# Four mixture-of-experts feed-forwards: the experts' weights are copied to all partitions by GpSimd instead of by a one-hot product

## What is computed

```python
comb = top_k_weights(x @ router)              # tokens x experts, zero outside the top 2 (L0: top 4 of 128)
for e in experts:                             # L1: 16, L2: 8, L3: 8; hidden width 128, 128, 176
    h = silu(x @ Wg[e]) * (x @ Wu[e])
    out += comb[:, e:e+1] * (h @ Wd[e])
out += shared(x)                              # the same without a weight; L2: weighted by a sigmoid gate
```

## Time and profile before

| | |
|---|---|
| time, median of 3 runs | 1829.1 us (1828.53 to 1836.51) |
| the profiled execution | 1830.67 us, span of its instructions 1828.8 us, mean granted TensorE clock 0.984 |
| TensorE, VectorE, ScalarE, GpSimd busy | 95%, 61%, 39%, 12% |
| L0's feed-forward | from 491.5 to 556.9 us |
| L1's | from 695.4 to 803.0 us |
| L2's | from 1195.0 to 1261.6 us |
| L3's, with the store | from 1741.7 to 1828.8 us |

### The profile page before, as it was taken

One profiled execution on the slowest core, in us unless ns is written; L12 is line 12 of the kernel. 1 busy time (PEld: TensorE's weight loads), 2 busy tenths in 40 slices (PEclk: granted clock), 3 DMA queues, 4 the chain that ended last, 5 costly groups with the idle time before them and its releaser, 6 DMA issues. The chain is left out here.

```text
span 1828.8 us, 35508 instructions
## 1 busy us (share of the span) xinstructions
PE 1732.9 (95%) x15270; PEld 1161.0 (63%) x15270; DVE 1106.8 (61%) x1938; ACT 720.3 (39%) x1213; POOL 218.0 (12%) x384
## 2 busy tenths in 40 slices
PE   8999999999998889998989999999999999999998
PEld 4584367777664655655447777755366757777755
DVE  1824578888456763245568888534455358888532
ACT  2222256666312331123246666411354246666411
POOL 0122500000000000000420000000166000000000
PEclk9999999999999889998999999998999999999999
DMA  6302010000210021040020000050200220000010
GB/s 213 112 1 94 1 70 2 2 2 2 87 84 1 2 76 37 1 147 18 1 87 2 2 2 2 2 233 3 52 7 1 104 82 2 2 2 2 2 56 10
DMA packets 11789, 73.45 MB, mean 40 GB/s; under 512 B 3483, under 2 KB 5019, under 8 KB 7125
## 3 DMA queue, kind: packets, MB, share of 16 engines
q1 hardware_dynamic: 11634, 71.19, 10.7%
HBM read 70.73 MB, written 0.46 MB: 39 GB/s over the span
## 5 line engine op out<-in xcount | busy, mean ns | idle before, releaser
L941 ACT ACTIVATE arena<-ps,softmax_stats 128x1500 f32<-128x1500 f32 x168 | 253.8, 1511 | 218.7 <-DVE softmax_stats L1004 216.5
L863 PEld LDWEIGHTS ps<-arena,ctx_pos 125*64 125x64 f32 x4608 | 222.3, 137 | 58.4 <-issue 57.6
L850 PE MATMUL ps<-ident,arena 64*125 64x64 f32 x4032 | 237.9, 270 | 12.9 <-ACT arena L941 8.0
L850 PEld LDWEIGHTS ps<-ident,arena 64*125 64x125 f32 x4032 | 228.7, 185 | 31.5 <-issue 30.5
L863 PE MATMUL ps<-arena,ctx_pos 125*64 125x128 f32 (+1 forms) x4608 | 240.5, 262 | 0.0
L781 PE MATMUL ps<-ctx_feat,arena 64*128 64x500 f32 x1008 | 232.2, 589 | 6.6 <-issue 3.3
L948 ACT COPY arena<-ps 125x512 f32<-125x512 f32 x336 | 172.5, 600 | 70.2 <-PE ps L850 70.2
L199 PE MATMUL ps<-arena 128*128 128x256 f32 x736 | 176.0, 386 | 8.7 <-DVE arena L1242 3.0
L1015 DVE TENSOR_SCALAR arena<-arena,softmax_stats 128x1500 f32<-128x1500 f32 x168 | 168.3, 1002 | 5.9
L199 PEld LDWEIGHTS ps<-arena 128*128 128x128 f32 x736 | 138.4, 191 | 47.1 <-issue 17.7
L1139 PE MATMUL ps<-x_feat,arena 128*128 128x448 f32 (+1 forms) x416 | 166.1, 544 | 0.0
(11 more groups left out here) (279 smaller groups left out, 1978.3 us busy)
## 6 DMA issues: line engine op xcount, KB each, us to landing
ctx_pos<-in_ctx SPq DMA_DIRECT2D x1, 3000.0 KB
arena<-in_L1f_gate SPq DMA_DIRECT2D x1, 2304.0 KB, 11.1
arena<-in_L1f_up SPq DMA_DIRECT2D x1, 2304.0 KB, 16.1
arena<-in_L1f_down SPq DMA_DIRECT2D x1, 2304.0 KB, 7.8
arena<-in_L0a_Wq SPq DMA_DIRECT2D x1, 2048.0 KB, 9.6
arena<-in_L0a_Wc SPq DMA_DIRECT2D x1, 2048.0 KB, 11.0
arena<-in_L0x_Wq SPq DMA_DIRECT2D x1, 2048.0 KB, 12.6
arena<-in_L0x_Wo SPq DMA_DIRECT2D x1, 2048.0 KB, 12.9
```

What stands on the lines that cost most here:

```text
L850: m = nc.tensor.transpose(c.ps[0:LP, turn_bank(i, k, r), n * 64:(n + 1) * 64], probs[i % 2][e][rows, l * LP:(l + 1) * LP], c.ident[rows, r ...
L863: m = nc.tensor.matmul(y[r * 64:(r + 1) * 64, lo:hi], c.ctx_pos[:, j, l, e, :], pT[i % 2][:, lo // 64:hi // 64, LT * e + l, :], start=(l = ...
L941: nc.scalar.activation(probs[i % 2][e].rearrange("p (k l) -> p k l", k=3), sc[e], ACT.Exp, bias=low[:, i % 4, e:e + 1], accum_out=total[:, ...
```

## The change

The one-hot products, the tables and their loads go. In their place:

- *Rounds of four.* comb (in L1 to L3) is laid out so that expert e has column 32 * (e % 4) of round e // 4, the rest being cleared once. Turning a round (four transposes, `widen(r)`) puts the weights of its four experts on partitions 0, 32, 64 and 96 of a PSUM bank, and VectorE copies it to SBUF (`wide_out(r)`). L1 has 4 rounds, L2 3, L3 2. In L0 comb is turned as before, and a round is one product of `mixed` (the mixing table with the same spacing) with combT; 2 rounds. Rounds 0 and 1 go ahead of the loop on TensorE, further ones behind `down(0)` and `down(1)`. On VectorE round 0 goes ahead of the first gated chunk and each further one behind one.
- *Copies by GpSimd.* For each weighted chunk one `partition_broadcast` copies the expert's row (448 columns, from partition 0, 32, 64 or 96) to the 128 partitions of one of several SBUF tiles (8, 13, 5 and 11 of them in L0 to L3). A chunk with two experts takes two, the second over the first partitions, after a wait for the first. A tile is used again when its chunk has been gated.
- VectorE's second multiplication reads that tile instead of PSUM.

```diff
+    experts = 8 if mixing else f.cols if kind == "L2" else E
+    R = (experts + 3) // 4
+    combT = c.at(W + 1920, NT)
+    wideT = [c.at(W + (1920 + 448 * r if r < 2 else 3680 + 448 * r), NT) for r in range(R)]
+    if mixing:
+        wideT = wideT[1:] + [c.at(W + 4576, NT)]
+        comb = c.at(22256, 512).rearrange("p (j e) -> p j e", j=J)
+        mixed = c.at(22000, 256).rearrange("p (r m) -> p r m", r=R)
+    else:
+        comb = c.at(22000, J * R * 128).rearrange("p (j r m) -> p j r m", j=J, r=R)
+    tiles = [c.at(at, NT) for at in f.tiles]
...
+
+        k = f.chunks[n][2]
+        a, b = (min((128 * k + p) // f.width, experts - 1) for p in (0, 127))
+        return [(b, 128)] + ([(a, f.width * (a + 1) - 128 * k)] if a != b else [])
...
-            nc.gpsimd.memset(comb, 0.0).then_inc(*padded.next())
+            nc.gpsimd.memset(mixed if mixing else comb, 0.0).then_inc(*padded.next())
...
+            for i, n in enumerate(weighted):
+                if i >= len(tiles):
+                    pool.wait_ge(hid_in.handle, hid_in.at(weighted[i - len(tiles)] + 1))
+                tile = tiles[i % len(tiles)]
+                for step, (e, rows) in enumerate(of_chunk(n)):
+                    pool.wait_ge(wide_in.handle, wide_in.at(e // 4 + 1))
+                    if step:
+                        pool.wait_ge(bc_half.handle, bc_half.last())
+                    row = 32 * (e % 4)
+                    nc.gpsimd.partition_broadcast(tile[0:rows], wideT[e // 4][row:row + 1], channels=rows).then_inc(
+                        *(bc_in if step + 1 == len(of_chunk(n)) else bc_half).next())
...
-            def weights(n):
-
-                if n in weighted:
-                    pe.wait_ge(combT_in.handle, combT_in.at(1))
-                    m = nc.tensor.matmul(c.ps[:, bank(n) + 2, 0:NT], spread[:, f.chunks[n][2], :], combT,
-                                         start=True, stop=True)
-                    m.then_inc(*bc_mm.next())
+            def widen(r):
+
+                if r >= 2:
+                    pe.wait_ge(wide_in.handle, wide_in.at(r - 1))
+                bank = c.ps[:, 7 - 3 * (r % 2), :]
+                if mixing:
+                    m = nc.tensor.matmul(bank[:, 0:NT], mixed[:, r, :], combT, start=True, stop=True)
+                else:
+                    for j in range(J):
+                        m = nc.tensor.transpose(bank[:, j * 128:(j + 1) * 128], comb[:, j, r, :], c.ident[:])
+                m.then_inc(*wide_mm.next())
...
             pe.wait_ge(comb_in.handle, comb_in.at(1))
-            for j in range(J):
-                t = nc.tensor.transpose(c.ps[:, 7, j * 128:(j + 1) * 128], comb[:, j, :], c.ident[:])
-            t.then_inc(*comb_t.next())
+            if mixing:
+                for j in range(J):
+                    t = nc.tensor.transpose(c.ps[:, 7, j * 128:(j + 1) * 128], comb[:, j, :], c.ident[:])
+                t.then_inc(*comb_t.next())
+                pe.wait_ge(combT_in.handle, combT_in.at(1))
+            widen(0)
+            widen(1)
             arrived_late()
-            weights(0)
-            weights(1)
             for n in range(N):
                 if n > 0 or not mixing:
                     down(n)
-                if n + 2 < N:
-                    if n > 0 or not mixing:
-                        gate_up(n + 2)
-                    weights(n + 2)
+                if 2 <= n + 2 < R:
+                    widen(n + 2)
+                if n + 2 < N and (n > 0 or not mixing):
+                    gate_up(n + 2)
...
                 dve.wait_ge(s.dve_chain.handle, s.dve_chain.last())
                 V.tensor_scalar(mix[:, 0:8], mix[:, 0:8], mix[:, 8:9], scale, ALU.mult, ALU.mult).then_inc(*s.dve_chain.next())
                 dve.wait_ge(s.dve_chain.handle, s.dve_chain.last())
-                V.tensor_copy(spread[:, 0:8, :], mix[:, 0:8].unsqueeze(2).broadcast_to([128, 8, 128])).then_inc(*s.dve_chain.next())
+                V.tensor_copy(mixed.rearrange("p r (g m) -> p r g m", g=4)[:, :, :, 0],
+                              mix[:, 0:8].rearrange("p (r g) -> p r g", r=R)).then_inc(*s.dve_chain.next())
...
                 if n in weighted:
                     V.tensor_tensor(sl, up, sl, ALU.mult).then_inc(*s.dve_chain.next())
                     dve.wait_ge(s.dve_chain.handle, s.dve_chain.last())
-                    dve.wait_ge(bc_mm.handle, bc_mm.at(weighted.index(n) + 1))
-                    V.tensor_tensor(h, valid(c.ps[0:m_, bank(n) + 2, 0:NT]), valid(sl), ALU.mult).then_inc(*hid_in.next())
+                    i = weighted.index(n)
+                    dve.wait_ge(bc_in.handle, bc_in.at(i + 1))
+                    V.tensor_tensor(h, valid(tiles[i % len(tiles)][0:m_]), valid(sl), ALU.mult).then_inc(*hid_in.next())
...
-            V.tensor_tensor(comb[:, :, 0:E], ex, spr(small[:, 12:16]), ALU.mult).then_inc(*comb_in.next())
+            if mixing:
+                V.tensor_tensor(comb, ex, spr(small[:, 12:16]), ALU.mult).then_inc(*comb_in.next())
+            else:
+                V.tensor_tensor(comb[:, :, 0:E // 4].rearrange("p j r (g m) -> p j r g m", g=4)[:, :, :, :, 0],
+                                ex.rearrange("p j (r g) -> p j r g", g=4),
+                                small[:, 12:16].rearrange("p (j r g) -> p j r g", r=1, g=1).broadcast_to([128, J, E // 4, 4]),
+                                ALU.mult).then_inc(*comb_in.next())
             dve.wait_ge(comb_in.handle, comb_in.last())
...
+            if mixing:
+                dve.wait_ge(comb_t.handle, comb_t.at(1))
+                V.tensor_copy(combT.rearrange("p (b t) -> p b t", b=B),
+                              c.ps[:, 7, :].rearrange("p (b t) -> p b t", b=B)[:, :, 0:T]).then_inc(*combT_in.next())
+                dve.wait_ge(combT_in.handle, combT_in.last())
...
+            def wide_out(r):
+                dve.wait_ge(wide_mm.handle, wide_mm.at(r + 1))
+                bank = c.ps[:, 7 - 3 * (r % 2), :]
+                V.tensor_copy(valid(wideT[r]), valid(bank[:, 0:NT]) if mixing else
+                              bank.rearrange("p (b t) -> p b t", b=B)[:, :, 0:T]).then_inc(*wide_in.next())
+
+            wide_out(0)
             for n in range(1 if mixing else 0, N):
                 gated(n)
+                r = n if mixing else n + 1
+                if r < R:
+                    wide_out(r)
             norm_vector(c, s, dve, last)
 
 
...
-                          29696, 32256, 34816, 3, 35584, 22000, 35840),
+                          29696, 32256, 34816, 3, 35584, 35840, 128, [27000 + 448 * i for i in range(6)] + [22784, 23232]),
-                          6144, 10752, 25780, 18, 32448, 30400, 32480),
+                          6144, 10752, 25780, 18, 32448, 32480, 128, [448 * i for i in range(13)]),
-                          29696, 32256, 34816, 10, 37376, 22000, 37400),
+                          29696, 32256, 34816, 10, 37376, 37400, 128, [27200 + 448 * i for i in range(5)]),
-                          29696, 33280, 0, 14, 37448, 22000, 24064),
+                          29696, 33280, 0, 14, 37448, 24064, 176, [8000 + 448 * i for i in range(11)]),
-    if name != "L0_ffn":
-        n = {"L1_ffn": 16, "L2_ffn": 10, "L3_ffn": 11}[name]
-        d["spread"] = (tag + "_spread", c.at(f.spread, n * 128))
-                    "L2_xattn_last": 2, "L3_xattn_first": 3, "L3_xattn_next": 1, "L3_xattn_last": 2, "L0_ffn": 5, "L1_ffn": 6, "L2_ffn": 4, "L2_ffn_late": 1, "L3_ffn": 3, "L3_ffn_late": 2,
+                    "L2_xattn_last": 2, "L3_xattn_first": 3, "L3_xattn_next": 1, "L3_xattn_last": 2, "L0_ffn": 5, "L1_ffn": 5, "L2_ffn": 4, "L3_ffn": 3, "L3_ffn_late": 1,
-                fl["L1_ffn"], "down", "router", "spread", "extra")))
+                fl["L1_ffn"], "down", "router", "extra")))
-            feed_forward(c, "L2_ffn", spec["L2_ffn"], pick(fl["L2_ffn"], "spread"),
+            feed_forward(c, "L2_ffn", spec["L2_ffn"], [],
-            feed_forward(c, "L3_ffn", spec["L3_ffn"], pick(fl["L3_ffn"], "spread", "down"), nothing, out)
+            feed_forward(c, "L3_ffn", spec["L3_ffn"], pick(fl["L3_ffn"], "down"), nothing, out)
```

More of the change, by code:

```diff
@@ L1060, with __init__ @@
 class Experts:
-    def __init__(self, cols, experts, top, chunks, gate_tiles, gate, up, down, downs, router, spread, extra):
+    def __init__(self, cols, experts, top, chunks, gate_tiles, gate, up, down, downs, router, extra, width, tiles):
         self.cols, self.experts, self.top, self.chunks = cols, experts, top, chunks
         self.hidden, self.gate, self.up, self.down, self.downs = gate_tiles, gate, up, down, downs
-        self.router, self.spread, self.extra = router, spread, extra
+        self.router, self.extra, self.width, self.tiles = router, extra, width, tiles
 def feed_forward(c, name, f, now, prefetch, store=None, meanwhile=None):
@@ L1073, in feed_forward @@
     kind, E, last = name[:2], f.experts, store is not None
+    mixing = kind == "L0"
```

(31 more changed lines are left out.)

## The result

The changed kernel took 1820.28 us (median of 4 runs, 1804.6 to 1823.68); the kernel before took 1832.8 us beside it (4 runs, 1828.53 to 1842.64). The ratio is 0.9896, with a 95% interval of 0.9847 to 0.9945. So it is faster, by 12.5 us and not by 26.7, and it lies above the range that ended at 1812. The profiled execution took 1821.77 us (span 1819.7), to be set beside 1830.67 of before: 8.9 us less.

The account below looks back on a forecast made before the run. TensorE, 95% busy, bounds the kernel: 31.5 - 1.9 (ends) - 1.5 (rounds) - 1.4 (L0) - 0.2 (L2) + 0.2 (L1 attention) = 26.7 us gained, so 1804.0 us profiled, 1802.4 median; range 1797 to 1812.

Parts of the forecast that it names:

- The products (31.5 us): Feed-forward loops: 42 of 45 one-hot products leave TensorE's path at 0.75 us each, 31.5 us gained.
- Ends and rounds (1.9, 1.5): TensorE waits 0.47 us at four stage ends, 1.9 lost; three later rounds at 0.5 us in L1 and L2, 1.5 lost.
- L0 (1.4): L0's start: VectorE must copy round 0's product before gated(1), so down(1) comes later; net 1.4 us lost.
- The copy's price: One GpSimd copy of 448 columns: taken as 0.6 us, from plain copies (0.58) and an all-reduce (14 at most).
- The 54 us: One GpSimd copy by the skill page's reduction figure; the change would then cost over 2 ms.
- L2's start (0.2 lost): First copy and one SBUF hold of 0.6 us before down(0): 0.2 us lost, between 0.4 gained and 0.8 lost.
- all three loads are hidden: GpSimd's code loads in L0, L2 and L3 finish before the first copy can start, by 3 us at least.
- rival (b): Code loads begin only when input is ready and land on the path: gain 13.4, 1815.7 us; 4%.
- The sum: Whole kernel: all terms give 26.7 us gained, from the profiled 1830.67 to 1804.0, or 1802.4 for the median.
- The likeliest case: Whole kernel: the forecast itself, 1802.4 us, 4 us either way for clock dips and L2's hold; 80%.
- rival (d): TensorE's clock dips once per feed-forward after new idle times, 6.4 us lost, 8 with a fifth: 1810.4 us; 7%.

Follow-up runs that it names:

- the first repetition: The changed kernel run once more with no edit: 1815.63 us (7 runs), ratio 0.9906.
- the last six: The changed kernel, unedited, run again beside the kernel before on one chip: 1804.12 us (6 runs), ratio 0.9861.
- eight copies: The changed kernel with each GpSimd copy made eight times in sequence, each waited for: 1959.47 us (one execution).

## Why the prediction was wrong, point by point

**The products (31.5 us).** Right: 4.74 us per chunk and nothing in the loop waits. L1's feed-forward shows it by itself: forecast 16 x 0.75 = 12.0, less 0.47 and two rounds, 10.5; measured 9.1 with a fall of the clock that before did not have, and 10.7 without one (107.62 to 96.88). L3: 11 x 0.75 less 0.47 is 7.8; measured 6.2 and another 1.7 of clock, 7.9.

**Ends and rounds (1.9, 1.5).** Right: 0.43 us at L3's end for 0.47, and 0.44 us for a round of L1 (four transposes at 703.42, the next gate products at 703.86) for 0.5.

**L0 (1.4).** Right: the stage is 3.3 us shorter, and 7 x 0.75 - 0.47 - 1.4 is 3.4. The timeline shows the order that I worked out, answering to the earlier trace rows:

```profile
506.00 1.77 PE L1177 MATMUL ps<-arena 128*128 128x448 f32 x4 [0.78 <-DVE arena L1343]
...
507.13 0.62 DVE L1350 COPY arena<-ps 128x448 f32<-128x448 f32 x1 [1.18 <-PE ps L1177]
507.67 0.62 DVE L1278 TENSOR_TENSOR arena<-ps,arena 128x448 f32<-128x448 f32 x1
...
508.34 1.99 PE L199 MATMUL ps<-arena 128*128 128x256 f32 x8 [0.57 <-DVE arena L1278]
```

**The copy's price.** Between the ends of 0.58 and 14 us I took 0.6, and it is 0.66: the plain copy was the right neighbour and the all-reduce the wrong one. The 54 us that the Trainium skill's figure for a reduction gave does not hold for this operation.

**L2's start (0.2 lost): wrong.** The sentence that all three loads are hidden, by 3 us at least, took the 5.86 us of an idle DMA for the price. In L0 and L3 the copies did wait for their input and not for the load, but by the forecast's own times L3 had 2.4 us to spare and not 3. At L2's start the queue is full of the next stage's weights, the load took 11.07, and VectorE waited 2.13 us. down(0) starts 14.49 us after the stage's first work (1182.45 to 1196.94) where it was 12.86 before: 1.6 us late, not 0.2. A fall of the clock followed, as costly as the one that the earlier trace rows show of before, though at another point of the stage. Windows:

```profile
1196.00:1198.00 2.00, 1.06 (x5) 0.90 (x6) 1.93 (x4) 0.00 (x0) 2.00 (x4) 0.95 1.00 426
1198.00:1200.00 2.00, 2.00 (x7) 1.54 (x6) 1.01 (x1) 0.00 (x0) 2.00 (x4) 0.50 0.96 410
1200.00:1202.00 2.00, 2.00 (x7) 1.27 (x6) 0.62 (x1) 0.00 (x0) 0.21 (x1) 0.69 1.06 442
```

This fall costs (0.05 + 0.50 + 0.31) x 2 = 1.7 us, and the earlier one, at 0.83 between 1184 and 1194, as much; before had one of the two. So 4.8 forecast for the stage less 1.4 and 1.7 is 1.7, which is what it gained. The idleness alone doesn't bring the fall: in the trace of the first repetition TensorE waited 3.41 us at the same point, and the clock stayed at 1.00 in the 4 us behind it. It was rival (b)'s mechanism in another form: not that the load starts late, but that it takes longer.

**The clock: the step that failed.** The sum started from the profiled execution of before and carried its lost clock (29.3 us over the span) over to the changed kernel as it was. The likeliest case gave 4 us either way "for the clock's dips, which move when the stages move", and rival (d) priced the clock as one small dip of 1.6 us for each new idle gap, 6.4 to 8 us, at 7%. The four runs of the result lost 42.7 us in the mean, 13.4 more than 29.3; added to the forecast of 1804.0 this gives 1817.4, and their mean is 1817.2. In the profiled execution it was 17.1 us more, of which 13.7 in one stretch of 27 us, in a stage that neither the change nor its idle gaps touch. The earlier trace rows showed the size of a short fall, and I had looked for no long one.

Rival (d)'s short falls came too, 5.1 us of them, but only L2's came behind a new wait. L1's and L3's came 2.5 and 1.7 us after the stage's start, where TensorE had been idle for some 0.46 us as before, and in two of the later traces L1 has none. The mean over all runs, 6.3 us, is near rival (d)'s price, and a single execution can be far from it. The changed kernel's runs at clocks of 0.983 or more have a mean of 1803.3 us, within 1 us of the forecast, and those at 0.973 to 0.975 lie at 1818.5 to 1823.7. Which of them fill a set of four runs is luck: the last six would have had their median, 1804.12, inside the range. The runs of before, 1828.5 to 1836.5 in only three, held the same warning.

**What stays open.** Why the clock falls for so long, and why the changed kernel meets it more often: 12 of 17 runs are at a clock of 0.981 or less, and 24 of 63 before. All seven traces of the changed kernel and its variants without more filler in L3's cross-attention have a fall of over 20 us, and neither of the two traces of the kernel before has. So a part of the 6.3 us may belong to the change; this is not decided, since runs of one session resembled each other (seven of seven low in the first repetition, two of six in the last), and no execution of the kernel before was traced in its low-clock group. What the traces show ahead of the fall in L3's cross-attention is the same in both kernels: TensorE idle for 0.46 us at the stage's start, then thin work (products of 64x64, with a filler product between). In the six traces with the fall in this place it came 2.6 to 3.8 us after the stage's first product. Whether it is a matter of when the stage starts was not shown.

## What to carry to other kernels

A TensorE product that only spreads a row over the partitions can go to an idle GpSimd at 0.66 us for 448 columns, and gives back its full slot as long as the copies of a chunk take less than the chunk. Before such a move is called hidden, look at what the DMA queues carry while GpSimd loads its code: the load took nearly twice as long under full queues, and one wait on the load queue took it off the path. And when a forecast is a change of a per cent or so, read the granted clock over the whole kernel before and after, not only around the edit, and widen the range by the longest fall that the spread of the runs allows.

## What the runs showed of the hardware that was not expected

- A fall of the granted clock to 1.2 GHz can last 27 to 31 us while TensorE is busy all the time (12.00 of 12.00 us in the windows above), in a stretch that begins with 64x64 products and then has mostly products of 64 columns; it costs 14 to 15 us. A short fall cost L1's feed-forward 1.7 us (98.57 and 96.88 us).
- The code load of GpSimd took 5.86 us with idle DMA engines and 11.07 us with engines 93% busy.
- A product of VectorE with both inputs in SBUF takes 0.63 us alone (1804.02 in the changed kernel's timeline) and 0.85 and 1.03 while GpSimd copies (1196.03 and 1197.98 above); for the first of them I had added 0.6 and it was 0.2. The Trainium skill, page "GPSIMD Engine Reference", section "Key points", names such a contention for two inputs in SBUF, and the trace agrees.
- Lost clock costs nothing where another engine sets the pace: with eight copies the clock was 0.78 over L3's feed-forward, and the stages' length still followed GpSimd's copies.
